# In an attention stage of eight groups: ranks and places of the last groups one step sooner, weight pieces split one per step

## The reference

```python
h = concat([tok(x), txt(x_txt)], axis=1)          # (32, 114, 256)
h = h + attn(layernorm(h))                        # Laplacian attention, causal
h = h + ffn(layernorm(h))                         # 8 experts, top 2 of each row, then a layernorm
# ffn: logits = x @ w_router.T ; top_vals, top_idx = top_k(logits, 2) ; rw = softmax(top_vals)
#      y_e = (silu(x @ w_gate_e.T) * (x @ w_up_e.T)) @ w_down_e.T ; out = sum_r rw_r * y_{idx_r}
```

## Time and profile before

| | us |
|---|---|
| median of 3 runs | 1121.9 (1121.77, 1121.9, 1126.06) |
| the profiled execution | 1125.7 |
| its span, first to last instruction | 1123.9 |
| granted TensorE clock, mean | 0.939 |
| busy: PE / DVE / ACT / POOL | 975.9 / 758.9 / 601.9 / 577.5 |

### The profile page before, as it was taken

The page is one execution under the profiler, slowest core; times in us unless marked ns, Lnnn a source line. Parts: engine busy times, 40 slices in busy tenths (PEclk is TensorE's granted clock), DMA queues, the critical chain, the costliest instruction groups (busy, mean ns, idle before and its releaser), DMA issues.

```text
span 1123.9 us, 20592 instructions
## 1 busy us (share of the span) xinstructions
PE 975.9 (87%) x5838; PEld 846.4 (75%) x5839; DVE 758.9 (68%) x1966; ACT 601.9 (54%) x1343; POOL 577.5 (51%) x630
## 2 busy tenths in 40 slices
PE   5878999999999999999898962499999999999910
PEld 4668999999999999998666652377777777777710
DVE  1666999999999998998678767244444444444447
ACT  1466776877788777666697753123223223223223
POOL 4523765567667766777627767232222222222236
PEclk8998999999999999999999975699999999999965
DMA  9451001000100000012168236133233333333263
GB/s 278 130 151 57 1 1 66 1 2 1 67 1 2 1 25 2 10 58 57 36 212 260 61 76 224 52 47 50 47 47 49 49 47 47 47 50 48 43 162 118
DMA packets 54733, 75.49 MB, mean 67 GB/s; under 512 B 9348, under 2 KB 46978, under 8 KB 52612
## 3 DMA queue, kind: packets, MB, share of 16 engines
q1 hardware_dynamic: 32680, 49.24, 14.5%
q0 software_dynamic: 16640, 18.53, 10.1%
q10 hardware_dynamic: 5340, 6.83, 2.2%
HBM read 45.38 MB, written 29.14 MB: 66 GB/s over the span
## 4 chain that ended last, share of the span: by engine, by line
PE 68%; DVE 10%; POOL 7%; DMA 5%; issue 4%; ACT 3%; SPq 2%; POOLq 0%; ACTq 0%; DVEq 0%
PE bank L1264 16%; PE bank L1580 10%; PE bank L1329 7%; PE bank L1557 6%; PE bank L1566 5%; PE bank L1565 4%; PE bank L1324 3%; POOL xrows L1174 3%; PE bank L1560 3%; PE bank L1572 2%; DMA xtok<-in_tok_emb,tokens_s 2%; PE bank L1312 2%; SPq L541 1%; POOL xtok L1052 1%; DVE arena_b L1736 1%
## 5 line engine op out<-in xcount | busy, mean ns | idle before, releaser
L1203 POOL DMA_INDIRECT yrows<-arena_b,dest_i x64 | 99.2, 1550 | 268.2 <-ACT arena_b L1009 260.3
L1736 DVE SCALAR_TENSOR_TENSOR arena_b<-bank,sml,arena_b 128x304 f32<-128x304 f32 (+2 forms) x384 | 195.3, 522 | 20.7 <-ACT arena_b L778 17.9
L1264 PE MATMUL bank<-xt_hi,w_hi 128*128 128x308 f32 x512 | 159.9, 312 | 4.6 <-DVE arena_b L1736 3.2
L1264 PE MATMUL bank<-xt_hi,w_lo 128*128 128x308 f32 x512 | 157.3, 307 | 0.0
L1264 PE MATMUL bank<-xt_lo,w_hi 128*128 128x308 f32 x512 | 156.9, 306 | 0.0
L2057 DVE TENSOR_TENSOR arena_b<-bank,arena_b 128x512 f32<-128x512 f32 x64 | 44.3, 691 | 140.5 <-PE bank L1566 76.7
L1090 POOL TENSOR_TENSOR u_halves<-arena_b,u_halves 128x308 fp32r<-128x308 f32 x128 | 109.8, 865 | 29.8 <-ACT arena_b L790 29.7
L1084 POOL TENSOR_TENSOR y_lo<-arena_b,y_hi 128x308 fp32r<-128x308 f32 x128 | 107.9, 857 | 27.2 <-ACT y_hi L802 27.0
L1264 PEld LDWEIGHTS bank<-xt_hi,w_hi 128*128 128x128 f32 x512 | 98.0, 191 | 5.4 <-DVE arena_b L1736 3.5
L1580 PE MATMUL bank<-arena_b 128*128 x384 | 98.7, 393 | 1.2 <-DVE arena_b L2073 0.9
L1264 PEld LDWEIGHTS bank<-xt_hi,w_lo 128*128 128x128 f32 x512 | 98.0, 191 | 0.0
(11 more groups left out here) (212 smaller groups left out, 2650.3 us busy)
## 6 DMA issues: line engine op xcount, KB each, us to landing
arena_b<-xrows SPq DMA_DIRECT2D x64, 129.5 KB, 2.1
wg_raw<-in_w_gate SPq DMA_DIRECT2D x4, 1024.0 KB, 7.1
yrows<-arena_b SPq DMA_DIRECT2D x1, 3648.0 KB, 18.7
h_all<-seq SPq DMA_DIRECT2D x8, 448.0 KB
w_raw<-in_w_in SPq DMA_DIRECT2D x3, 1024.0 KB, 4.8
arena_b<-in_w_down SPq DMA_DIRECT2D x3, 1024.0 KB, 8.6
wu_raw<-in_w_up SPq DMA_DIRECT2D x2, 1024.0 KB, 7.3
wu_s<-in_w_up SPq DMA_DIRECT2D x2, 1024.0 KB, 9.4
```

The source lines that it names most:

```text
L1203: pool.indirect_dma_start(yrows, bass.IndirectOffsetOnAxis(ap=dest_i[:, m:m + 1], axis=0), f_y[m % 2], None, compute_op=ALU.add).then_inc( ...
L1264: mm = pe.matmul(out_, in_half(w, layer, d, slice(c * P, (c + 1) * P)), x[:, d, cols], start=(k == 0), stop=(k == len(pairs) - 1))
L1736: dve.scalar_tensor_tensor(acc[:, :, back_:TXT], x[:, :, 0:TXT - back_], conv_w(s // GROUPS, c, tap), acc[:, :, back_:TXT], ALU.mult, ALU. ...
```

## The change

`ranks` and `place_rows` of groups 6 and 7 move from step g+3 to the end of step g+2 (group 5 stays where it was). `upper_weights` is called once in each of the steps 2 to 7 on ACT, between `norm_rows` and `weight`; `lower_weights` once in each of the steps 3 to 8 on DVE, between `norm_ahead_stats` and `choose`. No piece is left at its old place. The orders of POOL and SP are not touched.

```diff
-        SPLIT_FIRST = 3
+        SPLIT_FROM = 2
...
                 if has(g + 1):
                     norm_rows(g + 1)
+                if 0 <= g - SPLIT_FROM < len(FFN_HALVES):
+                    upper_weights(g - SPLIT_FROM)
                 if has(g - 2):
                     weight(g - 2)
...
                 if has(g):
                     gate_values(g, 1)
-                if g - 1 == GROUPS - 1:
-                    for k in range(SPLIT_FIRST):
-                        upper_weights(k)
                 if has(g - 1):
                     routed_norm(g - 1)
...
-            for k in range(SPLIT_FIRST, len(FFN_HALVES)):
-                upper_weights(k)
...
-                if has(g - 3):
+                if has(g - 3) and g <= GROUPS:
                     ranks(g - 3)
...
                 if has(g + 1):
                     bias_scores(g + 1)
+                if has(g - 2) and g >= GROUPS:
+                    ranks(g - 2)
...
-                if has(g - 3):
+                if has(g - 3) and g <= GROUPS:
                     place_rows(g - 3)
...
-                if g - 2 == GROUPS - 1:
-                    for k in range(SPLIT_FIRST):
-                        lower_weights(k)
+                if 0 <= g - 1 - SPLIT_FROM < len(FFN_HALVES):
+                    lower_weights(g - 1 - SPLIT_FROM)
                 if has(g - 2):
                     choose(g - 2)
...
                 if has(g - 1):
                     routed_bias(g - 1)
+                if has(g - 2) and g >= GROUPS:
+                    place_rows(g - 2)
...
             dve.wait_ge(tbl_ready, 2)
-            for k in range(SPLIT_FIRST, len(FFN_HALVES)):
-                lower_weights(k)
```

## The result

The changed kernel takes 1134.26 us (median of 6 runs, 1132.17 to 1136.32) against 1123.91 for the kernel before (6 runs on the same chip): a ratio of 1.0091, with a 95% interval of 1.0068 to 1.0115. The forecast was +8.1 us, slower (1130.0, range 1120 to 1136, from the 1121.9 known then); the medians say +10.4, inside the range. The profiled executions are 1134.63 and 1125.7.

What follows compares the result with a forecast made beforehand. Bound: POOL's queue of indirect sends between attention and experts, and inside attention a ring of engines, none full. Terms: 8.3 + 1.6 + 3.0 + 2.3 - 7.1 = +8.1, so 1121.9 + 8.1 = 1130.0 us, range 1120 to 1136.

Steps and rivals of the forecast that it cites:

- The stall: Step 2 on ACT: the first piece waits for its loads and holds the queue behind it, +8.3 us.
- The stall is no stall: Rival, step 2: loads land in time for ACT or the rings catch up; 1120.1 us, chance 0.13.
- The clock behind it: PE after the wait in step 2: idle drops it to the lower clock, work at half pace, +1.6 us.
- the sign: On PE in the profile after: turn_routed(1) would take 1.78 us, not 1.00.
- Long sends: Steps 3 to 7: a send starting inside DVE's piece ends 1.0 after it; +3.0 in 3 and 4, +2.3 in 5 to 7.
- Sends do not mind a lone piece: Rival, steps 3 to 7: only a row of pieces makes sends long; 5.3 us go, 1124.7, chance 0.12.
- "+2.3" for steps 5 to 7: Sends beside pieces there: +4.1 us, less POOL's idle of 1.3 and some 0.5 hidden by ACT's queue.
- a longer ring: Attention steps: a loop of engines waiting on one another, period 15.23 us in steps 3 and 4; lengthened sends lengthen it.
- More time at the low clock: Rival, steps 3 to 6: idler PE falls to half pace again, 1.6 us each, three give 1134.9; chance 0.14.
- The tail: Last 16 sends, groups 6 and 7: queue starts 2.1 us sooner and runs without pieces, -7.1 us.
- Nothing at the tail: Rival, after the last sends: padding or w_down lands later than they do; 7.1 us come back, 1137, chance 0.03.

Runs made afterwards that it cites:

- experiment 5: The kernel before, with only the first piece's ACT half (upper_weights(0)) moved to step 2: 1133.31 us, ratio 1.0085.
- experiment 3: The changed kernel with all pieces one step later (upper in steps 3 to 8, lower in steps 4 to 9): 1125.53 us, ratio 1.0001 against the kernel before.
- experiment 6: The changed kernel with each DVE half of a piece cut into four operations of 512 columns: 1128.12 us, ratio 1.0035 against the kernel before.
- experiment 4: The changed kernel with each DVE half replaced by a one-input sum over the same 2048 columns, lower halves zeroed: 1123.37 us, ratio 0.9992 against the kernel before.
- experiment 2: The changed kernel with ranks and place_rows of all groups back in step g+3, only pieces moved: 1134.31 us, ratio 1.0083 against the kernel before.
- Experiment 9: The kernel before, with two one-input sums over 632 columns on DVE ahead of routed_bias in steps 3 to 7: 1138.11 us, ratio 1.0129.
- Experiments 1: The kernel before, with only ranks and place_rows of groups 6 and 7 moved, pieces left at the end: 1119.77 us, ratio 0.9953.
- experiment 10: The changed kernel again, with no edit: 1132.32 us, ratio 1.0084 against the kernel before.
- experiments 4 and 7: The second of these: the changed kernel with pieces one step later and DVE halves in four operations: 1117.74 us, ratio 0.9939 against the kernel before.
- experiment 8: The changed kernel, upper pieces in steps 3 to 8, cut DVE halves in steps 5 to 8, last two meant behind POOL's sends: 1117.24 us, ratio 0.9938.

## Why the forecast was right, and where not

**The stall** (forecast +8.3, measured +7.75; +8.9 by itself in experiment 5, clock included) is right, by its mechanism and its place: SP's wait for the first loads, read in the earlier trace rows, was ACT's as well. The rival "The stall is no stall" fell with the 7.63 us in ACT's row and with experiment 3, in which it is gone. The size is not good to 1 us: over six profiles with the piece in step 2, ACT's idle is 5.82 (experiment 6), 7.42, 7.53, 7.63, 10.19 and 10.27. It hangs on when the loads land, against ACT's own work.

**The clock behind it** (+1.6, measured +1.2) is right in kind and wrong in whom it hits: values and bias_scores at half pace, and turn_routed(1), which I had named as the sign, at 1.00 already.

**Long sends** (+5.3 in the steps 3 to 7). One in each step, 2.3 to 2.7 us, ending 1.0 behind its piece: right. "Sends do not mind a lone piece" fell, and with it, for these sends, the rule that was set against the rows: the Trainium skill (SBUF — State Buffer, Who interferes with whom) infers that a tensor_tensor with two SBUF inputs leaves the writing of descriptors alone. Here six sends beside such an operation have 2.26 to 2.68 us, and with the one-input sum of the same duration in its place (experiment 4) the sends beside it go back to 1.12. Whether it is the writing of descriptors that waits or the send's reading of slot_i, no run tells. The steps with a long send and, but for 2.4 us of step 4, at the full clock have 16.74, 16.74, 15.08 and 15.96 (steps 4 to 7, experiment 2), those without one 15.18, 15.18, 14.45 and 15.22 (experiment 4): 4.5 for four steps. With the forecast's 1.4 for step 3, which has no undisturbed row, that is 5.9; from it goes 1.0, since the kernel before had a low stretch of 3.4 in its step 5 (16.13, not 15.18). So some 4.9 are the long sends', for 5.3.

**The term that came out too small** is that of steps 3 to 7 as a whole: +5.3 forecast, +8.5 measured, and in it above all "+2.3" for steps 5 to 7, which took 4.65. The working knew a longer ring only as a longer ring. What was missing is some 3.6 us (8.5 less 4.9) of half-pace work in the low stretches from 609.7 and 643.9. That was a rival of its own, "More time at the low clock", to which I gave 0.14 and against which I held that the fall in the earlier trace rows had 4.02 of idle in one piece. Experiment 9 shows that it needs no such idle: 7.6 us spread over five steps brought 20 us more at the low clock, and PE's idle in front of turn_routed was just 2.34 at 609.48 and 2.31 at 643.92, where the clock fell both times. So the forecast and that rival came true together; the rival's figure for one fall (1.6) times two is near the 3.6. (Three such falls make 1134.8 by the prediction's own terms, not 1134.9.)

**The tail** (-7.1, measured -7.26) is right in both parts: the queue starts 2.1 sooner (step 8, -2.08), and sixteen sends without a piece take 21.52 for 21.6. Experiments 1 and 2 show the first part apart (2.3 and 2.4). The last landing and load, for which I had no change, took 0.37 more; 4.06 for 3.58 us is the send's own. "Nothing at the tail" fell.

**The sum** was 8.1 and is 10.6 in the profiles, 10.4 in the medians: 3.2 more came in steps 3 to 7 and 0.4 in the landing, 0.9 less in step 2, and the tail gave 0.2 more. The stall's size was partly luck: in experiment 10, the same kernel, group 0 was sent 2.65 us later than in this profile.

## What to carry to other kernels

Before work is moved ahead into an engine's hand-written order, look when its input lands: an engine that is idle for a third of a stage still blocks all that is queued behind the wait, and here 8 us of it came through a whole stage undiminished. Work that is put beside indirect sends costs by its form more than by its length; cut into short operations it cost the sends 0.5 us or less each, but for one, and an operation of the same length that reads one operand of SBUF cost them nothing. One step later and in four pieces the split made this kernel 0.6% faster than before where the change had made it 0.9% slower. Where a stage is a ring of engines that wait for one another, a delay may cost more than its length, here nearly twice, since TensorE can lose its clock with it.

## What the hardware showed unexpectedly

- **A longer ring loses the clock.** 7.6 us of delay in five steps cost 14.8, and the low stretches grew from 3.4 to 23.8 us (experiment 9). Where the pieces cost the ring little (experiments 4 and 7) PE went through 70 us of the same work at the full clock; before the change it had one stretch of 3.4. What makes the clock fall at one place and not at another is open: with 2.34 us of idle in front of turn_routed it fell, in the change, in experiment 10 and in experiment 2 (at 610.88 there), and with 2.30 in front of the one at 645.41 in experiment 2 it did not.
- **A send is held by the operation, not by the piece.** A send that starts inside a DVE operation with two SBUF inputs ends 1.0 us behind that operation's end, whether that took 2.26 us or about a quarter of it. The kind matters: a one-input sum of the same length (2.25) held none, nor did a tensor_tensor with one of its inputs in PSUM (experiment 4). One send beside cut pieces waited for all four (experiment 6), and that stays open.
- **An increment on POOL came ahead of its sends.** Written behind the last indirect send, it had been seen by DVE 9 us before that send started in the trace (experiment 8). It does not mark their end. The kernel's own wait for them, on SP, goes by the semaphores that the sends' DMAs raise.
- **The landing of the first loads varies.** In the chain of waits the first pair takes 9.1 to 9.3 us in four of the six profiles with the piece in step 2, and 11.6 and 11.7 in the two where ACT stood idle 10.2 and 10.3, with the same order of issue. The shortest stall, 5.8 in experiment 6, is not a faster load (9.15): there SP issued it 1.7 us ahead of norm_rows(3), and within 0.3 us of it in the others.
